# Moving a 16-byte buffer of a transformer block, so that two groups of tiles shift by 32 bytes against the weights

## The reference

```
x = x + 0.5 * ffn(layernorm(x))
x = x + attention(layernorm(x))
x = x + 0.5 * ffn(layernorm(x))
```

## Time and profile before

| | us |
|---|---|
| median of 3 runs | 2163.37 |
| lowest and highest | 2160.79, 2165.04 |
| the profiled execution | 2162.2 |
| its span, first to last instruction | 2160.5 |
| TensorE busy (98%) | 2126.9 |
| VectorE busy (66%) | 1430.4 |
| ScalarE busy (48%) | 1032.1 |

### The profile page before, as it was taken

How to read it: one execution, slowest core, us unless ns; L and a number is a source line. 1 busy time by engine, 2 the same in 40 slices (tenths; PEclk the granted TensorE clock), 3 DMA queues, 4 the chain that set the end, 5 groups by cost and what they waited for, 6 DMA issues and landing times.

```text
span 2160.5 us, 38424 instructions
## 1 busy us (share of the span) xinstructions
PE 2126.9 (98%) x14228; PEld 1951.2 (90%) x14228; DVE 1430.4 (66%) x3137; ACT 1032.1 (48%) x2006; POOL 468.8 (22%) x443
## 2 busy tenths in 40 slices
PE   8999999999999999999999999999999999999999
PEld 6888899999998788888888888888999999988888
DVE  7666646666664788888898986666566666633333
ACT  3333335555553666666666663333355555532222
POOL 3423211212122222222224322432112121200000
PEclk9999999999999999999999999999999999999999
DMA  9231225564445000000101101322244444441010
GB/s 272 89 121 58 74 67 137 129 153 99 101 112 153 20 1 20 21 20 1 36 1 57 38 11 63 116 71 68 70 103 104 109 104 104 110 135 59 30 59 20
DMA packets 194602, 168.41 MB, mean 78 GB/s; under 512 B 17017, under 2 KB 175149, under 8 KB 194416
## 3 DMA queue, kind: packets, MB, share of 16 engines
q1 hardware_dynamic: 176752, 144.57, 22.3%
q0 software_dynamic: 17664, 21.38, 5.6%
HBM read 104.32 MB, written 68.07 MB: 80 GB/s over the span
## 4 chain that ended last, share of the span: by engine, by line
PE 85%; DVE 9%; issue 3%; ACT 1%; DMA 1%; SPq 1%; POOL 0%; DVEq 0%; ACTq 0%; POOLq 0%
PE gate_up_p L339 28%; PE quad L339 24%; PE out_p L377 21%; PE misc L377 4%; PE misc L512 2%; PE quad L529 1%; DVE p_s L1176 1%; PE quad L543 1%; PE misc L403 1%; DVE smax L1172 1%; DVE h_s L1042 1%; PE misc L395 1%; PE misc L414 1%; DVE y_s L1185 1%; PE misc L412 1%
## 5 line engine op out<-in xcount | busy, mean ns | idle before, releaser
L339 PE MATMUL gate_up_p<-zh,w 128*128 128x512 f32 (+2 forms) x2368 | 705.0, 360 | 2.8 <-DVE h_s L1042 2.3
L713 ACT CAST hh<-h_s 128x512 fp32r<-128x512 f32 (+2 forms) x511 | 276.2, 540 | 682.9 <-DVE h_s L1042 673.2
L339 PE MATMUL quad<-zh,w 128*128 128x512 f32 (+2 forms) x1728 | 482.8, 347 | 0.0
L339 PEld LDWEIGHTS gate_up_p<-zh,w 128*128 128x128 f32 x2368 | 429.1, 188 | 51.7 <-DVE h_s L1042 3.8
L377 PE MATMUL out_p<-w,hh 128*128 128x256 f32 x2808 | 456.2, 281 | 2.4 <-DVE hl L1058 1.8
L377 PEld LDWEIGHTS out_p<-w,hh 128*128 128x128 f32 x2808 | 402.1, 189 | 21.1 <-DVE hl L1058 3.1
L339 PE MATMUL gate_up_p<-zl,w 128*128 128x512 f32 (+2 forms) x1184 | 420.8, 355 | 0.0
L1042 DVE TENSOR_TENSOR h_s<-gate_up_p,sg_s 128x512 f32<-128x512 f32 (+2 forms) x296 | 178.4, 603 | 247.9 <-PE gate_up_p L339 233.2
L1058 DVE TENSOR_TENSOR hl<-h_s,hh 128x512 fp32r<-128x512 f32 (+2 forms) x431 | 248.1, 576 | 136.3 <-ACT hh L713 120.8
L339 PEld LDWEIGHTS quad<-zh,w 128*128 128x128 f32 x1728 | 309.2, 188 | 24.8
L339 PE MATMUL quad<-zl,w 128*128 128x512 f32 (+2 forms) x864 | 295.8, 342 | 0.0
(11 more groups left out here) (201 smaller groups left out, 2757.7 us busy)
## 6 DMA issues: line engine op xcount, KB each, us to landing
stage<-in_L_ffn_rg SPq DMA_DIRECT2D x128, 128.0 KB, 2.8
stage<-in_L_ffn_ru SPq DMA_DIRECT2D x128, 128.0 KB, 3.0
stage<-in_L_ffn_rd SPq DMA_DIRECT2D x128, 128.0 KB, 3.0
slots_d<-empty SPq DMA_DIRECT2D x16, 662.5 KB, 6.9
zh_d<-zh SPq DMA_DIRECT2D x16, 512.0 KB, 3.2
zl_d<-zl SPq DMA_DIRECT2D x16, 512.0 KB, 4.4
y_d<-x SPq DMA_DIRECT2D x16, 512.0 KB, 5.7
zh<-zh_d SPq DMA_DIRECT2D x16, 512.0 KB, 4.2
```

The source lines that it names most:

```text
L339: last = pe.matmul(dst, a, b, start=(k == 0), stop=(k == 3 * n - 1))
L713: nc.scalar.copy(hh[:, n % 2, 0:ncol], h_s[:, n % 2, 0:ncol]).then_inc(sm["hh_done"], 1)
```

## The change

The declaration of lnd moves from the small tiles ahead of z to a place behind hl. Everything between the two places starts 32 bytes lower: the small tiles from lnm on, zh, zl, sg_s, h_s, hh and hl. zn, w0 and all behind it stay, and so do x, w1, stage and the constants ahead. z and h lie 32 bytes past the start of the weights modulo 512 instead of 64. The instructions on every engine, their order and their waits are the same.

```diff
@@ -95,7 +95,6 @@
         router_s = sb("router_s", [P, KC, E], F32)
         mhalf = sb("mhalf", [P, NT], F32)
         st = sb("st", [P, BT, 6], F32)
-        lnd = sb("lnd", [P, BT], F32)
         lnm = sb("lnm", [P, BT], F32)
         lnv = sb("lnv", [P, BT], F32)
         lndd = sb("lndd", [P, BT], F32)
@@ -138,6 +137,7 @@
         h_s = sb("h_s", [P, 2, SB], F32)
         hh = sb("hh", [P, 2, SB], F32R)
         hl = sb("hl", [P, 2, SB], F32R)
+        lnd = sb("lnd", [P, BT], F32)
         zn = sb("zn", [P, 2, BT, ROW], F32)
 
         sb("pad_w0", [P, 40], F32)
```

## The result

The change makes the kernel slower. Its median is 2182.5 us (2179.1 to 2184.1, 4 runs) against 2162.2 (2160.8 to 2165.0, 4 runs) for the kernel before: a ratio of 1.0088, 95% interval 1.0076 to 1.0100, or 19 us. The profiled execution took 2184.0 us with a span of 2182.2, 21.7 more than the span before.

A forecast was written before the change was run, and what follows sets the result against it. TensorE's matmul intervals were taken to bound the kernel; of 37 us that operand distance could give back, about half would go: 2162.2 - 19 + 1.2 = 2144.4, rounded to 2144 us, range 2125 to 2181.

The forecast's parts named there:

- What bounds the kernel: Whole kernel: TensorE is busy 2126.9 of 2160.5 us, so time can change only in the interval between matmul starts.
- if it grew by a tenth, is 2 us: Other engines and DMAs: half of TensorE's 33.6 us of idle time, growing by a tenth, would cost 2 us.
- The regimes: Gate, up and down: same matmuls run at two intervals 4 ns apart, read as the two operand streams hindering each other.
- The terms: Gate, up and down: time above streaming plus 2.3 ns, 11.7 + 8.0 + 4.0 + 13.5 us, total 37 us.
- that any distance could give back: Gate, up and down: upper bound of the gain from any operand distance, 37 us or 1.7% of the run.
- The step that failed: Gate, up and down: the regime is chosen anew in each group, giving back about half of 37 us, 19 us.
- the slow regime: 256-column matmuls: the longer interval, 6.5 to 7 ns above streaming cost, where the fast one lies some 2.3 ns above.
- 25 us more: Gate, up and down: loss if everything ran in the slow regime and 512-column matmuls at 231 to 232 ns.
- slower, because near is worse: Rival, gate, up and down: hindrance grows as streams come closer in address; 2174 to 2185, taken 2179; chance 0.27 including other costs.
- Nothing changes: Rival, TensorE intervals: the regime depends on when a group begins, not on addresses; 2163 us, chance 0.29.
- Alignment: Gate and up: streams starting in mid-block may need one more access each, 2.7 us at most over 6144 matmuls.

The follow-up runs named there:

- a single series: Separate kernel, TensorE alone: 24 equal matmuls per distance between moving and stationary operand; 512 columns ran at 226.7 to 234.3 ns.
- the best one found: Full kernel with z at 60 and h at 88 bytes past the weights, against the kernel before: 2158.8 us, ratio 0.9980.
- the bare chunks: Separate kernel, feed-forward matmuls alone on TensorE in the kernel's order, no waits, 64 pairs of z and h distances; 64/64 fastest, second and third chunks 1730.7 and 1726.3 us.

## Why the prediction was wrong

**What bounds the kernel** held: TensorE's intervals carry the whole difference, its waits none of it, and the other engines are busy as long as before. Of the idle time that "if it grew by a tenth, is 2 us" nothing grew.

**The regimes** were seen rightly: 113 to 114 and 118 ns at 256 columns exist at equal residues, and a single series has either, 113.3 or 117.7, by its distance alone, with no other engine at work. That the difference "depends on how the two streams stand to each other in time or address" is now shown for the address; that it is also a matter of time is argued, from one product's pace changing with the other's addresses. What in the chip makes it so, and why the period is 256 bytes, stays open.

**The terms** of the possible gain were too large. I took 0.434 ns a column plus 2.3 ns for a floor: 113.4, 169.0 and 224.5 ns. At 256 columns that is right, the fastest steady series ran at 113.3. At 384 and 512 columns the fastest ran at 173.3 and 226.7, the latter the same 0.443 ns a column as 113.3 at 256. And no layout gave every product its own best: of the 37 us "that any distance could give back" the best one found gave 4.

**The step that failed** is the sign. "Today 384s and most downs stand in the slow one, and so the more of them have something to gain" assumed that what I called the slow regime was about the worst, so that a new distance would give back half of the 37 us. The runs show that it is not. The 384s stood at 173.9 ns, near the bottom of the 172.9 to 177.7 that the bare chunks have on their 64 pairs; they went to 175.8 with the change, 2.11 us for twelve where I had forecast 2.04, and to 176.5 at a distance of 96. The 512s went from 229.6 to 232.6, to 233.6 at 96, and to 237.7 with z at 68; down went from 116.2 to 118.2. There are not two regimes but many patterns, and each of the others tried at 32-byte steps was worse in the full kernel: 0, 32, 96, 128 and 256 for both, and 32 for either alone. That 64 was so good a place could not be read from the trace of before.

The other end of the same sum came close to what happened. "25 us more" was 8.3 + 3.1 + 3.4 + 10.0; measured from the averages, 9.2 + 2.9 + 0.9 + 10.0. As a bound it isn't safe, since 96 cost 26 us. And the range ended at 2181, short of it and of the 2185 that the rival of nearness reached to; 2182.5 lies above.

**The rival "slower, because near is worse"** had the number, 2179, and a false reason. 96, 128 and 256 are further away and slow. Its evidence, 120 ns in the v product at distance 0, was true: the kernel with z and h at 0 has 119.8 ns at 256 columns, and so has the one at 256. I should have read it as one more distance with a value of its own. That the rival came within 4 us is luck.

**"Nothing changes"** falls too. Its argument, the projection at 192 and down at 64 with the same two values, is explained by the period: the weights stream 192 bytes behind the y tiles there, which modulo 256 is 64 ahead, gate's own distance. The trace of before held three distances and not four, and the third, 0, was the slow one at 256 columns. The Trainium skill's statement, on the page "TensorE: Matmul & The Clock Gate", section "Step-by-step: what each phase is for", that a weight load takes no read bandwidth from the running matmul, cannot be read here as saying that the two don't affect each other. With nothing but the distance between them changed, a single series of 512 columns ran at 226.7 to 234.3 ns, 3%, and those of the full kernel at 229.2 to 237.7. Whether it is read bandwidth that is lost, no run shows.

**Alignment** ("2.7 us at most") cost nothing that could be measured: ratio 0.9997 with all of z, h and the weights at odd multiples of 32.

## What to carry to other kernels

In this kernel, where TensorE streams four-byte operands back to back, the address of the moving tile relative to the stationary one, modulo 256, is a tuning parameter worth about 1%, and a layout edit made for another reason can cost as much. Neither a single series nor a rule of thumb foretold it. A small kernel with the real order of matmuls and no waits measures all pairs in one run, to within 10 to 15 us here, and then the two or three best are timed in the full kernel. When a profile shows the same instruction at two steady intervals, that says that something the profile doesn't name is at work, not that there is something to gain.

## What the runs showed that I had not expected

- At the lower clock the effect is gone: 426 to 427 ns for a 512-column matmul at every distance tried in the full kernel, against 228.5 to 237.7 at the upper level.
- The effect has a period of 256 bytes: tiles 256 apart give the same interval to 0.1 ns in the full kernel (119.8 and 119.8, 119.4 and 119.4) and within 0.01 us in 8.4 for the single series.
- Four bytes matter: z at 64 and at 68 differ by 18 us in the full kernel, 229.6 against 237.7 ns for a 512-column matmul.
- 512- and 256-column matmuls want different distances: in a single series at 0 they run at 226.7 and 120.0 ns, with the moving operand 64 bytes behind at 233.3 and 113.3.
- Weight loads beside 16-column matmuls follow each other at 111.7 ns at every distance; the effect needs a longer stream beside them.
- One product's pace depends on the other's addresses: moving z alone raised down, whose addresses were untouched, from 116.2 to 117.2 ns.
